# Building the stacked image of a bilinear tap convolution: on which engine and in what order its parts are copied

## What is computed

```python
xp = jnp.pad(x, ((0, 0), (0, 0), (PAD, PAD), (PAD, PAD)))
taps = [_bilinear_tap(xp, tap_offsets[k, 0], tap_offsets[k, 1], H_out, W_out) for k in range(K)]
g = jnp.stack(taps, 0)                                  # 9 taps, at offsets (i + 0.4, j + 0.4)
return jnp.einsum('kbiyx,oik->boyx', g, weights)        # 32 channels in, 32 out
```

## Time and profile before

| what | value |
|---|---|
| median of 3 runs | 394.69 us (394.27 to 398.84) |
| the profiled execution's own time | 394.71 us |
| its span, first to last instruction | 392.8 us |
| TensorE busy | 368.4 us, 94% of the span |
| VectorE, ScalarE, GpSimd busy | 260.9, 60.2, 97.7 us |
| mean granted TensorE clock | 0.982 of full |
| chain that ended last: TensorE, VectorE, DMA | 86%, 7%, 2% |

### The profile page before, as it was taken

One profiled execution on the slowest core, in us unless ns is written; L12 is line 12 of the kernel. 1 busy time (PEld: TensorE's weight loads), 2 busy tenths in 40 slices (PEclk: granted clock), 3 DMA queues, 4 the chain that ended last, 5 costly groups with the idle time before them and its releaser, 6 DMA issues.

```text
span 392.8 us, 8970 instructions
## 1 busy us (share of the span) xinstructions
PE 368.4 (94%) x3446; PEld 261.1 (66%) x3446; DVE 260.9 (66%) x469; ACT 60.2 (15%) x129; POOL 97.7 (25%) x248
## 2 busy tenths in 40 slices
PE   4799999999999999999999999799999979799991
PEld 3557888888888888888888887323366742466670
DVE  4675777877878878878788788434425376902255
ACT  1125010010100100101001000420041029442200
POOL 4527777888600000000000000114010019400000
PEclk9999999999999999999999999889999989999998
DMA  7654847527357076173481000489600000000032
GB/s 225 167 138 121 202 119 194 153 53 199 98 127 200 23 187 160 47 199 101 117 204 26 0 0 0 105 183 217 126 2 3 2 1 2 0 3 5 3 108 110
DMA packets 28641, 38.59 MB, mean 98 GB/s; under 512 B 7072, under 2 KB 23776, under 8 KB 27936
## 3 DMA queue, kind: packets, MB, share of 16 engines
q1 hardware_dynamic: 18080, 27.52, 27.6%
q10 hardware_dynamic: 10528, 10.61, 10.4%
HBM read 4.56 MB, written 2.10 MB: 17 GB/s over the span
## 4 chain that ended last, share of the span: by engine, by line
PE 86%; DVE 7%; DMA 2%; ACTq 1%; issue 1%; ACT 1%; SPq 0%; POOL 0%; DVEq 0%; POOLq 0%
PE ps L866 23%; PE ps L867 23%; PE ps L870 8%; PE ps L917 8%; PE ps L1056 5%; PE ps L1040 5%; PE ps L901 4%; PE ps L985 3%; PE ps L1009 2%; DMA X<-in_x 2%; PE ps L841 2%; ACTq L374 1%; PE ps L1025 1%; PE ps L930 1%; PE ps L975 1%
## 5 line engine op out<-in xcount | busy, mean ns | idle before, releaser
L866 PE MATMUL ps<-WA,HS 128*128 128x512 f32 x384 | 153.6, 400 | 0.7 <-DVE TS L1121 0.7
L867 PE MATMUL ps<-WB,LS 128*128 128x512 f32 x384 | 150.7, 392 | 0.0
L1143 DVE TENSOR_TENSOR PROD<-ps,PT 128x512 f32<-128x512 f32 x128 | 88.4, 691 | 39.2 <-PE ps L870 33.4
L1127 DVE TENSOR_REDUCE RED<-PROD 128x32 f32<-128x512 f32 x128 | 86.4, 676 | 0.0
L866 PEld LDWEIGHTS ps<-WA,HS 128*128 128x128 f32 x384 | 72.4, 189 | 19.2 <-issue 0.9
L867 PEld LDWEIGHTS ps<-WB,LS 128*128 128x128 f32 x384 | 72.4, 189 | 14.9
L870 PE MATMUL ps<-WC,TS 96*128 96x512 f32 x128 | 50.6, 395 | 0.0
L482 POOL MEMSET IMG<- 128x67 f32 x1 | 0.2, 154 | 139.4 <-DVE X L1133 139.4
L901 PE MATMUL ps<-REPL,ONE 128*128 128x256 f32 x120 | 29.4, 398 | 1.7 <-DVE X L1328 1.3
L724 ACT ACTIVATE HS<-HS 32x40 fp32r<-32x40 f32 x21 | 5.7, 274 | 164.3 <-DMA TS<-LO 164.0
L917 PE MATMUL ps<-SK,WE 128*32 128x512 f32 x256 | 30.0, 628 | 0.0
(11 more groups left out here) (223 smaller groups left out, 335.0 us busy)
## 6 DMA issues: line engine op xcount, KB each, us to landing
LS<-HS SPq DMA_DIRECT2D x7, 960.0 KB, 5.8
HS<-HI SPq DMA_DIRECT2D x60, 80.0 KB, 2.5
SK<-IMG SPq DMA_DIRECT2D x32, 131.8 KB, 2.6
HS<-LO ACTq DMA_DIRECT2D x32, 80.0 KB, 2.7
LS<-LO ACTq DMA_DIRECT2D x32, 80.0 KB, 2.7
HS<-HI SPq DMA_DIRECT2D x30, 79.8 KB, 2.6
TS<-LO SPq DMA_DIRECT2D x34, 63.8 KB, 4.0
out_x<-OT SPq DMA_DIRECT2D x8, 256.0 KB, 2.1
```

What stands on the lines that cost most here:

```text
L866: pe.matmul(ps[b][:, :], px(HS, dy), WA[:, dy, :], start=(dy == 0), stop=False)
L867: pe.matmul(ps[b][:, :], px(LS, dy), WB[:, dy, :], start=False, stop=False)
L1127: ve.tensor_reduce(RED[j % 2][:, 32 * b:32 * b + 32], PROD[b % 2][:, :].rearrange("p (o e) -> p o e", e=E0), AX.X, ALU.add).then_inc(sum_d ...
L1143: ve.tensor_tensor(PROD[b % 2][:, :].rearrange("p (o e) -> p o e", e=E0), ps[b][:, :].rearrange("p (o e) -> p o e", e=E0), para.broadcast_ ...
```

## The change

PIECES keeps sizes of 8, 8, 8 and 3 rows but in that order, where before it was 8, 3, 8, 8. Pieces 0, 2 and 3 go to banks 4 to 7, piece 1 to banks 0 to 3, so that a piece waits for the copies of the piece before the last one (piece 2 for those of piece 0, piece 3 for those of piece 2) and piece 1 for none. Chunk 0 still waits for two pieces, now 16 rows. VectorE's first stretch of IMG grows from 10 to 15 rows, ScalarE's second falls from 16 to 11. The DMA parts leave out the transfers with g = b, whose source and target are the same partitions: 12 transfers a part in place of 16. ScalarE makes these with `copy_same`: four copies of 32 partitions for each part, part 0 between its share of piece 2 and that of piece 3, parts 1 and 2 behind its DMA issues of part 2. Those no longer wait for chunk 2. Chunks 3, 5 and 7 wait for `stack1_same` as well.

```diff
--- before.py
+++ after.py
@@ -81,7 +81,9 @@
 Z_LATER = Z_IMAGE + 3
 
 
-PIECES = ((0, 8), (8, 11), (11, 19), (19, 27))
+PIECES = ((0, 8), (8, 16), (16, 24), (24, 27))
+PIECE_BANK = (4, 0, 4, 4)
+NORM_V = 15
 STACK_DMA = ((27, 43), (43, 59), (59, 67))
 IMG_V = 40
 RELU_ROWS = ((8, 16), (16, 24), (24, 32), (32, 40), (40, 48), (48, 56), (56, H - 1), (6, 8))
@@ -250,6 +252,7 @@
         stack1_by_vector = sem("stack1_by_vector")
         stack1_by_scalar = sem("stack1_by_scalar")
         stack1_by_dma = [sem(f"stack1_by_dma{i}") for i in range(len(STACK_DMA))]
+        stack1_same = sem("stack1_same")
         conv1_done = sem("conv1_done")
         x2_done = sem("x2_done")
         norm2_done = sem("norm2_done")
@@ -339,8 +342,9 @@
         def stack_piece(b, r0, r1):
             return SK[:, b, r0 * PW:r1 * PW].rearrange("p (r c) -> p r c", c=PW)[:, :, 0:W]
 
-        def copied_piece(b, r0, r1):
-            return ps[4 + b][:, 0:(r1 - r0) * W].rearrange("p (r c) -> p r c", c=W)
+        def copied_piece(n, b):
+            r0, r1 = PIECES[n]
+            return ps[PIECE_BANK[n] + b][:, 0:(r1 - r0) * W].rearrange("p (r c) -> p r c", c=W)
 
         def copy_rows(queue, part):
 
@@ -348,7 +352,8 @@
             a, n = r0 * PW, (r1 - r0 - 1) * PW + W
             for b in range(B):
                 for g in range(4):
-                    queue.dma_start(SK[32 * g:32 * g + 32, b, a:a + n], IMG[32 * b:32 * b + 32, a + g:a + g + n]).then_inc(stack1_by_dma[part], 16)
+                    if g != b:
+                        queue.dma_start(SK[32 * g:32 * g + 32, b, a:a + n], IMG[32 * b:32 * b + 32, a + g:a + g + n]).then_inc(stack1_by_dma[part], 16)
 
         def relu_px(i):
             r0, r1 = RELU_ROWS[i]
@@ -741,17 +746,29 @@
                                       bias=NMR[p, 0:1], scale=RS[p, 0:1])
 
             act.wait_ge(coef_ready, 1)
-            for r0, r1 in ((26, 42), (10, 26)):
+            for r0, r1 in ((26, 42), (NORM_V, 26)):
                 norm(rows(IMG, 1 + r0, r1 - r0), r0, r1).then_inc(image_by_scalar, 1)
+
+            def copy_same(part):
+
+                r0, r1 = STACK_DMA[part]
+                for b in range(B):
+                    ins = act.activation(stack_piece(b, r0, r1)[32 * b:32 * b + 32], image_piece(b, r0, r1, b), ACT.Copy)
+                ins.then_inc(stack1_same, 1)
+
             for n, (r0, r1) in enumerate(PIECES):
+                if n == 3:
+                    act.wait_ge(zeroed, Z_IMAGE)
+                    act.wait_ge(image_by_vector, 2)
+                    act.wait_ge(image_by_scalar, 2)
+                    copy_same(0)
                 act.wait_ge(stack_copied, n + 1)
                 for b in (2, 3):
-                    ins = act.activation(stack_piece(b, r0, r1), copied_piece(b, r0, r1), ACT.Copy)
+                    ins = act.activation(stack_piece(b, r0, r1), copied_piece(n, b), ACT.Copy)
                 ins.then_inc(stack1_by_scalar, 1)
-            act.wait_ge(zeroed, Z_IMAGE)
-            act.wait_ge(image_by_vector, 2)
-            act.wait_ge(conv1_done, 3)
             copy_rows(act, 2)
+            copy_same(1)
+            copy_same(2)
 
             act.wait_ge(coef_ready, 2)
             act.wait_ge(zeroed, Z_LATER)
@@ -921,13 +938,13 @@
             def copy_piece(n):
 
                 r0, r1 = PIECES[n]
-                if n:
-                    pe.wait_ge(stack1_by_vector, n)
-                    pe.wait_ge(stack1_by_scalar, n)
+                if n >= 2:
+                    pe.wait_ge(stack1_by_vector, 2 * n - 3)
+                    pe.wait_ge(stack1_by_scalar, 2 * n - 3)
                 for b in range(B):
                     p = slice(32 * b, 32 * b + 32)
                     for g in range(4):
-                        ins = pe.matmul(ps[4 + b][32 * g:32 * g + 32, 0:(r1 - r0) * W], REPL[p, 0, :], image_piece(b, r0, r1, g), start=True, stop=True)
+                        ins = pe.matmul(ps[PIECE_BANK[n] + b][32 * g:32 * g + 32, 0:(r1 - r0) * W], REPL[p, 0, :], image_piece(b, r0, r1, g), start=True, stop=True)
                 ins.then_inc(stack_copied, 1)
 
             pe.wait_ge(x1_done, NCH)
@@ -944,7 +961,8 @@
                     pe.wait_ge(stack1_by_vector, k + 2)
                     pe.wait_ge(stack1_by_scalar, k + 2)
                 if k in (3, 5, 7):
-                    pe.wait_ge(stack1_by_dma[k // 2 - 1], 16 * 16)
+                    pe.wait_ge(stack1_by_dma[k // 2 - 1], 16 * 12)
+                    pe.wait_ge(stack1_same, k // 2)
                 if k >= 4:
                     pe.wait_ge(x2_done, k - 3)
                 conv(k, lambda y: WE[:, y, :], 4, conv1_done)
@@ -1173,12 +1191,12 @@
                                         MV[p, 0:1], RS[p, 0:1], ALU.subtract, ALU.mult)
 
             coefs(2)
-            norm(rows(IMG, 1, 10), 0, 10).then_inc(image_by_vector, 1)
+            norm(rows(IMG, 1, NORM_V), 0, NORM_V).then_inc(image_by_vector, 1)
             norm(rows(IMG, 43, H - 42), 42, H).then_inc(image_by_vector, 1)
             for i, (r0, r1) in enumerate(PIECES):
                 ve.wait_ge(stack_copied, i + 1)
                 for b in (0, 1):
-                    ins = ve.tensor_copy(stack_piece(b, r0, r1), copied_piece(b, r0, r1))
+                    ins = ve.tensor_copy(stack_piece(b, r0, r1), copied_piece(i, b))
                 ins.then_inc(stack1_by_vector, 1)
 
             ve.wait_ge(far_known, 1)
```

## The result

The changed kernel takes 393.39 us in the median of 19 executions (390.6 to 395.5), the kernel before 396.41 us in the median of 19 (392.85 to 400.42). The ratio is 0.9942, 95% interval 0.992 to 0.9964. Forecast were 390.0 us, in 388.4 to 393.0, and 4.7 us less than before, 1.2%: the time lies above the range, and the gain is smaller than forecast by either measure.

The account below looks back on a forecast made before the run. It took TensorE's waits and slow clock in the bilinear block as the bound: 394.71 us less 4.9 (1.85 of waits, 3.0 of clock) plus 0.2 for chunk 5 gave 390.0 us, range 388.4 to 393.0.

Parts of the forecast that it names:

- The pieces: TensorE's pieces ahead of chunk 0: waits of 0.58 us in place of 2.43, a gain of 1.85 us.
- The clock: TensorE from piece 2 through chunk 0: the clock stays at full speed, a gain of 3.0 us.
- The change hides nothing: Chunks 3 to 7 never waited for the 16 removed transfers, so replacing them is worth 0; no chance of its own.
- the wait at chunk 5: Ahead of chunk 5: part 1 lands just in time; 0.2 us of waiting put into the sum.
- ScalarE: ScalarE's queue: four copies 3.8 us, 12 issues 7.6 us; `copy_same(1)` done at 269.7, 1 us before chunk 5.
- the third rival: Slower than before: `copy_same(1)` stands behind 12 ScalarE issues, at 2.04 us each 14.6 us late, 404.4 us; chance 0.05.
- The second rival: Part 1 comes late to chunk 5 because two queues share 205 GB/s: 391 to 394 us; chance 0.11.
- rows 3: Clock windows of the kernel before: read as 1.2 GHz from a third into 252 to 253 until just after 259.
- The first rival: The clock falls all the same in the block, only 1.85 us of waits are won: 392.8 us; chance 0.14.
- The second fall of the clock: Low clock in the 33rd slice, near 320 us: up to 1.35 us won or lost if it moves, not in the sum.

Follow-up runs that it names:

- pieces_only: Changed kernel with all 16 transfers a part, no ScalarE copies, part 2 behind chunk 2: 397.52 us, ratio 1.0044 to the kernel before; traced again, 398.28 us (one).
- before_third: Kernel before, no edit, traced a third time: 402.01 us (one execution).
- fills_before: Kernel before with fillers (3 and 1) in its two waits between pieces: 397.77 us, ratio 1.0073.
- before_again: Kernel before, no edit, measured beside itself with a second trace: 396.02 us, ratio 1.0071.
- part2_on_sync: Changed kernel with ScalarE only copying and SyncE issuing part 2 behind part 1: 391.58 us, ratio 0.9912 to the kernel before.

## Why the prediction was wrong

**Right:** VectorE's norm is hidden (by 0.14 us, not by the 0.6 reckoned; 1.27 us in place of 0.78). The pieces: 0.37 and practically 0 us of waits in place of 1.53 and 0.90; chunk 0 3.86 us after piece 0, forecast 3.96. The clock stays up from 248 to 282 in the trace, and the 3-row piece and its copies are hidden. Copy durations: 1.06 us, forecast 1.03, but in a row none hides a part of the next: four take 4.26 us, taken as 3.8. Chunk 5 is ready 22.0 us after piece 0, forecast 21.8.

**The mechanism that failed** is the step under *The change hides nothing*: "replacing them is worth 0. The gain is that of the pieces alone." It was argued from the 24.25 us without a gap. But a wait that isn't there says only that TensorE was later than the transfers, not by how much. Chunk 5 came 26.7 us after piece 0, and 32 issues of 0.71 us with 2.7 for landing are 22.8 + 2.7 = 25.5 us, by rows that stood in the prediction. The 2.7 was the median; the last transfer took 3.8 us, and part 1 landed 26.1 us after piece 0, 0.6 us before TensorE was ready for it. In the second trace of the kernel before it was so close that the weight load of chunk 5 waited for it:

```profile
...
273.67 0.13 PEld L917 LDWEIGHTS ps<-SK,WE 128*32 128x32 f32 x4 [0.31 <-DMA SK<-IMG]
...
```

pieces_only shows the rest: ready at 22.0 us, 3.79 waited. So the gain needed both halves, and the transfers' removal was no trifle but the condition of it. This step doesn't enter the sum, since the changed kernel has both halves.

**The term of the sum that failed** is the wait at chunk 5, set at 0.2 us and measured at 0.80, 1.19 and 1.60. What was mis-sized stands under *ScalarE*. `copy_same(1)` was forecast to end 20.9 us after piece 0, 1 us early, and ended at 22.7, 23.1 and 23.5. In the first trace ScalarE's issues began 1.2 us sooner than reckoned, but the 12 took 10.1 us in place of 7.6, and the four copies 4.3 in place of 3.8. This is the third rival's place, at 0.8 to 1.6 us of wait where it priced 14.6. The second rival was there too: part 1 was forecast to land 21.8 us after piece 0, with 1.9 us for the sharing, and landed at 22.5, 22.8 and 22.0. The prediction had "beside SyncE's transfers ScalarE's issues kept to 0.64" and 267 GB/s for two issuers. In the kernel before the two queues issued together for 2.8 us only. In the changed kernel ScalarE's first five issues kept to 0.64 us as well; then, with 8 or 9 transfers issued and not yet landed, its next seven took 0.67 to 1.45 us, 0.97 in the mean. The 2.04 us of SyncE needn't have been a full queue, as the third rival read it: in the changed kernel SyncE's third issue took 1.58 us with only two transfers under way. And over 260 to 267 us all transfers moved 225 GB/s, hardly more than with one issuer before (columns as in the earlier trace rows, the changed kernel first):

```profile
...
260.00:267.00 7.00, 7.00 (x71) 2.15 (x67) 2.77 (x4) 0.00 (x0) 4.29 (x2) 1.00 0.97 225
...
```

```profile
...
260.00:267.00 7.00, 7.00 (x92) 2.00 (x88) 3.96 (x6) 1.09 (x2) 3.72 (x3) 1.00 0.93 208
...
```

**The clock** was counted as a loss of 3.0 us that a full clock gives back. The slow clock hid the transfers. In the profiled execution itself part 1 landed at 26.1 us, so by my estimate a full clock with the old transfers would have brought chunk 5 forward by 0.6 us, not 3.0. In before_third, without the fall, chunk 5 waits 3.05 us, and in fills_before 2.85. Nor does the fall last 6.8 us each time (3.4 in before_again). The reading of rows 3 was also loose: the clock fell at 252.3 us, so 0.7 of the 2.43 us of waits came behind the fall, not ahead of it. The first rival (the clock falls all the same) is refuted by all three traces of the changed kernel.

**How the miss adds up.** 393.39 is 3.4 us above 390.0. Of these 1.7 are the level: the median before was 394.69 of 3 executions, and 396.41 of 19. No reading of the trace would have given it; a range around a median of three should have been wider on the upper side, since one of the three was 398.84. The other 1.7 are the gain's, 3.0 us by the medians in place of 4.7. About 1.0 of it is the wait at chunk 5 (1.2 in the mean of three traces, 0.2 in the sum). The remaining 0.7 isn't traced to a step. The block of before is 37.10, 35.68 and 39.14 us, that of the changed kernel 33.31 to 34.03, forecast 32.4. On each of three occasions the means of all executions of the two kernels differ by 2.6 to 3.4 us (without one execution of 740 us), and the ratio gives 2.3 us (0.58% of 396.4). How the gain splits between waits and clock in a mean execution isn't settled by three traces. The second fall of the clock, put at up to 1.35 us in either direction, came in the changed kernel at 313, 320 and 337 us. Its single times go with the mean granted clock, so such falls are the likely cause of its spread; no run separates them.

The Trainium skill, page "DMA: Bandwidth & Descriptors", section "Issuing engines are not separate DMA queues", says that transfers issued by several engines interleave on the same 16 DMA engines. The trace bears this out more than I allowed: both issuers slowed down (ScalarE from 0.64 to 0.92 us an issue, SyncE from 0.71 to 0.81, 19.38 us for 24, in part by slow single issues that come with SyncE alone too), and the 270 GB/s of the window at 259.1 to 260.6 us didn't last. The section adds that a second issuer saves only issue time; part2_on_sync, with one issuer, ended its block as early (32.19 us).

## What to carry to other kernels

A timeline without a gap ahead of a step doesn't mean that the step's other inputs are early: work out for each when it arrives, and take the smallest lead as the most that speeding up the first can win. Where several inputs come close together, an edit that speeds up one of them measures as nothing until the next one is sped up as well. A rate or an issue time read where two queues overlap for 3 us needn't hold where they overlap for 10. A slow clock ahead of a step whose other input is late anyway costs little, so test its worth by fillers before counting it. On an engine that both computes and issues DMAs, put the copies that others wait for ahead of the issues.

## What was not expected of the hardware

- At chunk 5 the granted clock fell to 1.2 GHz during or behind every wait of 2.85 to 5.96 us (before_third, fills_before, pieces_only, pieces_only_2), and behind none of 0.16 to 1.66 us.
- One kernel met the low clock at other places from execution to execution: before at 252 us for 6.8 us, at 253 for 3.4 us, and in the third trace not until chunk 5 had waited, at 277 us.
- A DMA issue on ScalarE took 0.52 to 0.64 us in the first 3.1 us in which both queues issued, and 0.97 us in the mean of the seven that followed. What this cost SyncE is less sure: its 24 issues took 18.5 to 19.7 us in the three traces of the changed kernel, but 16.5 to 18.6 in the orders where ScalarE issues later, where two or three of them took 0.9 to 1.9 us each.
- VectorE's norm of 960 elements took 1267 ns where those of 640 and 1408 took 609 and 1008; those of 256 and 2560 (410 and 1608 ns in the trace of before) lie on the same line, 0.52 ns an element above 276. 960 elements are 15 rows, the only odd number of rows among them, and took twice as long an element. Whether that is the cause wasn't tested.
